# Cross-attention values by seven products of quarters in a Perceiver block on one core

## The reference

```python
q = (query @ Wq + bq).reshape(b, sq, 16, 64)      # query = layernorm(x)
k = (key @ Wk + bk).reshape(b, 512, 16, 64)       # key = value = ctx_1024
v = (value @ Wv + bv).reshape(b, 512, 16, 64)     # Wq, Wk, Wv: 512 x 1024
scores = jnp.einsum('bqhd,bkhd->bhqk', q, k) / 8
attn = jax.nn.softmax(scores, axis=-1)
out = jnp.einsum('bhqk,bkhd->bqhd', attn, v).reshape(b, sq, 1024)
out = out @ Wo + bo + query                       # then a layernorm
```

## Time and profile before

| | |
|---|---|
| median of three runs | 1711.32 us (1709.48 to 1712.38) |
| the profiled execution | 1711.51 us, its span 1709.7 us |
| TensorE busy, of the span | 94% |
| VectorE, ScalarE, GpSimd busy | 68%, 55%, 18% |
| mean granted clock of TensorE | 0.976 |
| first attention's loop | about 75 to 955 us |

### The profile page before, as it was taken

How to read it: one execution, slowest core, us unless ns; L and a number is a source line. 1 busy time by engine, 2 the same in 40 slices (tenths; PEclk the granted TensorE clock), 3 DMA queues, 4 the chain that set the end, 5 groups by cost and what they waited for, 6 DMA issues and landing times. The chain is left out here.

```text
span 1709.7 us, 27478 instructions
## 1 busy us (share of the span) xinstructions
PE 1615.2 (94%) x10730; PEld 1361.0 (80%) x10730; DVE 1163.9 (68%) x1978; ACT 938.0 (55%) x1700; POOL 307.3 (18%) x258
## 2 busy tenths in 40 slices
PE   7999999999999999999999878994899999999987
PEld 6888888888888888888887766773788888888876
DVE  4277777877777777777777666775768448548842
ACT  5466666666666666666666433442656336336631
POOL 4201211011101110111100161565311011101101
PEclk9999999999999999999999999996999999999899
DMA  6601830111101110111002560114757437528711
GB/s 228 212 24 54 131 77 7 54 57 54 37 27 53 57 54 8 54 56 54 7 5 80 173 187 14 55 57 138 249 150 212 141 87 242 155 89 247 221 39 21
DMA packets 54107, 165.21 MB, mean 97 GB/s; under 512 B 10612, under 2 KB 10996, under 8 KB 53408
## 3 DMA queue, kind: packets, MB, share of 16 engines
q1 hardware_dynamic: 38032, 131.88, 22.6%
q0 software_dynamic: 15920, 31.19, 8.7%
HBM read 143.54 MB, written 55.64 MB: 117 GB/s over the span
## 5 line engine op out<-in xcount | busy, mean ns | idle before, releaser
L413 PE MATMUL psum<-ctx,Wk 128*128 128x512 f32 x1536 | 386.2, 400 | 0.0
L413 PE MATMUL psum<-Wv,ctx 128*128 128x512 f32 x1536 | 368.7, 389 | 0.0
L413 PEld LDWEIGHTS psum<-Wv,ctx 128*128 128x128 f32 x1536 | 288.3, 188 | 59.9
L413 PEld LDWEIGHTS psum<-ctx,Wk 128*128 128x128 f32 x1536 | 280.1, 189 | 55.9
L932 DVE SCALAR_TENSOR_TENSOR kT<-psum,bkc,kT 64x512 fp32r<-64x512 f32 x256 | 191.9, 750 | 170.0 <-ACT kT L1322 165.8
L413 PE MATMUL psum<-xgT,Wh 128*128 128x224 f32 (+5 forms) x1536 | 250.0, 316 | 15.1 <-issue 10.2
L413 PEld LDWEIGHTS psum<-xgT,Wh 128*128 128x128 f32 x1536 | 228.4, 196 | 32.7 <-issue 12.6
L766 PE MATMUL psum<-Wh,hs 128*128 128x512 f32 x981 | 245.6, 396 | 0.0
L1332 ACT ACTIVATE Pr<-Pr,smn 128x512 f32<-128x512 f32 x128 | 92.6, 724 | 233.9 <-DVE smn L941 233.9
L1322 ACT ACTIVATE kT<-psum,bkc 64x512 fp32r<-64x512 f32 x256 | 175.1, 684 | 77.7 <-PE psum L413 73.8
L766 PEld LDWEIGHTS psum<-Wh,hs 128*128 128x128 f32 x981 | 181.1, 190 | 33.7 <-DVE hs L1207 0.3
(11 more groups left out here) (154 smaller groups left out, 1911.1 us busy)
## 6 DMA issues: line engine op xcount, KB each, us to landing
raw<-in_W SPq DMA_DIRECT2D x128, 512.0 KB, 4.3
expert_rows<-in_spare_rows SPq DMA_DIRECT2D x16, 1042.0 KB, 7.3
raw<-in_ctxT SPq DMA_DIRECT2D x32, 512.0 KB, 4.4
xg<-expert_rows POOLq DMA_DIRECT2D x32, 256.0 KB, 5.9
low_parts<-Olo POOLq DMA_DIRECT2D x32, 128.0 KB, 2.4
oT<-low_parts SPq DMA_DIRECT2D x8, 512.0 KB, 4.3
out_x<-x SPq DMA_DIRECT2D x12, 256.0 KB, 2.2
xs<-in_x SPq DMA_DIRECT2D x4, 512.0 KB, 6.8
```

The costliest lines, as they stand in the source:

```text
L413: mm = pe.matmul(dst, l, r, start=n == 0, stop=n == len(pairs) - 1)
```

## The change

The values of a batch, 512 keys x 1024 dims, are no longer eight tiles of twelve matmuls. Context and Wv are cut into quarters (256 keys x 256 dims, 256 dims x 512), and each half of the keys' tiles (p = 0, 1; G = 2b + p) gets seven products P1 to P7 of two blocks, six matmuls each, after Strassen and Winograd. Their operands are quarters and sums of quarters: S1 to S4 of the context, made for each batch, and T1 to T4 of Wv, made once, each split in a high and a low part.

- TensorE takes them in the order P1, P6 (in steps with n % 4 = 2), P2, P7 (3), P4, P5 (0), P3 (1), behind `weigh`, alternating between two PSUM banks. No values are projected ahead of the loop.
- ScalarE copies P1 out of PSUM (`move_v`), VectorE adds the others up in the value tiles (`evict_v`): one sum for P6, P2, P7, P4 and P3, two for P5, seven per G. The sums stand ahead of the reciprocal in VectorE's step, as the eviction did.
- VectorE no longer scales the probabilities: ScalarE does, at the end of its step, waiting for the reciprocal (`s_recip`).
- The values have no bias in them. It is added when the weighed output is evicted, in four pieces of 128x64 each on ScalarE (high part, `Ohr`) and VectorE (low part).
- Both parts of the output go to DRAM (`high_parts` beside `low_parts`) and come back by `high_part` and `low_part`, since the keys' weights now lie where `Ohi` is.
- The queries go to DRAM through four staging tiles `qst` (`q_rows`) and come back per batch (`fetch_qb`, `qb`); the score operand is built in halves of a batch, eight copies of 64x256 per batch.
- GpSimd makes S1 to S4 (`ctx_sums`) and their low parts (`sums_low`), eight operations of 128x512 per batch; ScalarE makes their high parts (`sums_high`, in steps with n % 8 = 4, 6 and 7). At the start VectorE and ScalarE do the same for the first batch and for Wv, and VectorE takes over GpSimd's splits there.
- The experts: the first chunk of `weighted` waits for all chunks of its expert but for the last expert's, GpSimd issues a filler copy for each chunk that an expert doesn't have, and the exponential of the router's last tile (`d_gate`) stands ahead of a weight split.

```diff
-        QO = place("QO", c0, [P, NJ, T])
...
+        VW = {name: [place(f"{name}{i}", c0 + kb + 4 * i, [P, 2, 512], F32R) for i in range(2)]
+              for name, kb in (("T1", 32), ("T4", 40), ("B22", 56), ("B11", 64), ("T2", 72), ("B21", 80), ("T3", 88))}
+        qst = [place(f"qst{r}", c0 + 48 + 2 * r, [P, 512]) for r in range(4)]
+        qb = [place(f"qb{r}", c0 + 48 + 2 * r, [P, NJ, TB]) for r in range(2)]
+        Ohr = [place(f"Ohr{r}", c0 + 52 + r, [P, NJ // 2, TB], F32R) for r in range(4)]
...
+        def v_products(n):
+
+            if n < 2:
+                return ((0, "P1"), (0, "P6")) if n == 0 else ((0, "P2"), (0, "P7"), (0, "P4"), (0, "P5"))
+            G, names = {2: ((n + 2) // 4, ("P1", "P6")), 3: ((n + 1) // 4, ("P2", "P7")), 0: (n // 4, ("P4", "P5")), 1: ((n - 1) // 4, ("P3",))}[n % 4]
+            return (((0, "P3"),) if n == 2 else ()) + (tuple((G, name) for name in names) if G < NG else ())
...
+                if t < 2:
+                    sp.wait_ge(v_psum, 7 * NG - 1)
+                    dst = oH[t][:]
+                else:
+                    sp.wait_ge(k_psum, NS)
+                    dst = Ohi[:, :, t * P:(t + 1) * P]
+                sp.dma_start(dst.bitcast(F32), high_parts[t]).then_inc(low_in[t % 4], 16)
...
+                elif name == "P7":
+                    pe.wait_ge(s_lo, 4 * b + 2)
+                    pe.wait_ge(v_done, 7 * G + 1)
+                    left, right = key_tile(CS["S3"], p), "T3"
...
-                products(v_bank(n), split_pairs([pair(ctx[b % 2], slice(None), k, ks) for k in range(KD)],
-                                                      [pair(Wv, slice(None), k, cs) for k in range(KD)])).then_inc(v_psum, 1)
+                    pe.wait_ge(s_lo, 4 * b + 4)
+                    pe.wait_ge(v_done, 7 * G + 4)
+                    left, right = key_tile(CS["S4"], p), "B22"
+                pairs = split_pairs(left, [[VW[right][i][:, kk, :] for i in range(2)] for kk in range(2)])
+                mm = products(v_bank(G, name), pairs)
+                mm.then_inc(v_psum, 1)
...
-            for n in range(HALF):
-                project_v(n)
             for n in range(NS + 3):
                 if n < NS:
                     project_k(n)
                 if 0 <= n - 1 < NS:
                     scores(n - 1)
-                if n + HALF < NS:
-                    project_v(n + HALF)
                 if n >= 6 and n % HALF == 2:
                     weigh(n // HALF - 1)
+                for G, name in v_products(n):
+                    project_v(G, name)
...
+                if name == "P6":
+                    v.wait_ge(v_moved, G + 1)
+                    if v_room(G):
+                        v.wait_ge(o_psum, v_room(G))
+                    v.tensor_tensor(v_tile(G, 0, 1), src, v_tile(G, 1, 0), ALU.add).then_inc(v_done, 1)
...
+                elif name == "P5":
+                    v.wait_ge(v_done, n + 4)
+                    v.tensor_tensor(v_tile(G, 1, 1), src, v_tile(G, 1, 1), ALU.add).then_inc(v_done, 1)
+                    v.tensor_tensor(v_tile(G, 0, 1), src, v_tile(G, 0, 1), ALU.add).then_inc(v_done, 1)
...
-                if n + HALF < NS:
-                    evict_v(n + HALF)
+                for G, name in v_products(n):
+                    evict_v(G, name)
                 if n >= 1:
                     v.wait_ge(s_exp, 3 * m + 3)
                     v.reciprocal(srec[:, r:r + 1], ssum[:, r:r + 1]).then_inc(s_recip, 1)
-                    v.wait_ge(s_recip, m + 1)
-                    v.tensor_scalar(Pr[m % 2][:], Pr[m % 2][:], srec[:, r:r + 1], None, ALU.mult).then_inc(p_done, 1)
-                if j == 2 and b + 1 < B:
-                    build_qbd(b + 1)
+                if n % HALF == 2 and n // HALF + 1 < NS // HALF:
+                    build_qbd(n // HALF + 1)
...
+                    if n >= 4:
+                        s.wait_ge(q_out[n % 4], 16 * (n // 4))
+                    s.activation(qst[n % 4][:], bank[2 + n % 6], ACT.Identity, bias=bqs[:, j:j + 1], scale=SCALE1).then_inc(q_done, 1)
...
+                        s.activation(qs[h][u % 2][dst, :, own], qb[b % 2][own, HALF * half:HALF * (half + 1), :], ACT.Copy).then_inc(qbd_hi, 1)
...
+                for s_ in range(HALF):
+                    high = s.activation(Ohr[u % 4][:, s_, :], bank[7][:, s_ * TB:(s_ + 1) * TB], ACT.Identity,
+                                        bias=bvc[:, HALF * half + s_:HALF * half + s_ + 1])
+                high.then_inc(o_hi, 1)
...
+                    s.activation(v_tile(G, 1, 0), v_bank(G, name), ACT.Copy).then_inc(v_moved, 1)
...
+                for G, name in v_products(n):
+                    move_v(G, name)
+                if n % HALF == 2 and n // HALF + 1 < NS // HALF:
+                    build_qbd(n // HALF + 1)
...
+                if 0 <= n - 1 < NS:
+                    m, r = n - 1, (n - 1) % 3
+                    s.wait_ge(s_recip, m + 1)
+                    s.activation(Pr[m % 2][:], Pr[m % 2][:], ACT.Copy, scale=srec[:, r:r + 1]).then_inc(p_done, 1)
+                if n < NS and b + 1 < B and j in (4, 6, 7):
+                    sums_high(b + 1, {4: ("S2", "S3"), 6: ("S1",), 7: ("S4",)}[j])
...
             x2_turned(NT - 1)
+            d_gate(NT - 1)
             split_first(3)
-            d_gate(NT - 1)
...
+            def ctx_sums(b):
+
+                x0, x1_ = (raw[raw_of[sum_load(b, c)]][:].rearrange("p (a b) -> p a b", a=2) for c in range(2))
+                n = 4 * b
+                g.wait_ge(s_lo, n - 1)
+                g.tensor_tensor(tS[0][:], x0[:, :, 256:512], x1_[:, :, 256:512], ALU.add).then_inc(s_sum, 1)
...
+                    g.wait_ge(s_hi, 4 * b + i + 1)
+                    g.tensor_tensor(CS[name][1][:], src[:], CS[name][0][:], ALU.subtract).then_inc(s_lo, 1)
...
+                g.dma_start(q_rows[n // NJ, n % NJ], qst[n % 4][:]).then_inc(q_out[n % 4], 16)
...
+                for parts, x in ((high_parts, Ohr), (low_parts, Olo)):
+                    g.dma_start(parts[b // 2, :, HALF * half:HALF * (half + 1), b % 2 * TB:(b % 2 + 1) * TB], x[u % 4][:].bitcast(F32)
+                                ).then_inc(low_out[u % 4], 16)
...
-                        v.wait_ge(y_ready, q + c + 1)
+                        v.wait_ge(y_ready, c + 1)
                     elif c == 0:
-                        v.wait_ge(y_ready, q + 1 if q < E else q + CH)
-                    else:
                         v.wait_ge(y_psum, NI * (q + 1))
```

More of the change, by code:

```diff
@@ L62, in perceiver_block @@
         bkc = small("bkc", [P, NJ])
+        bvc = small("bvc", [P, NJ])
         mv = small("mv", [P, NT, 2])
@@ L193, in ctx_load, with sum_load, hi_turn, v_bank @@
             return (L_CTX0 if b == 0 else L_CTX + 2 * (b - 1)) + c
+        def sum_load(b, c):
+            return (L_S0 if b == 0 else L_CTX + 2 * (b - 1)) + c
+        def hi_turn(n):
+            return n + 1 if n < L_WV else n + 1 - (L_CTX - L_WV)
+        VK = (0, 2, 1, 3)
+        NG = 2 * B
+        V_ORDER = ("P1", "P6", "P2", "P7", "P4", "P5", "P3")
+        def v_bank(G, name):
+            return bank[2 + (7 * G + V_ORDER.index(name)) % 2]
+        v_slot = [{}]
+        for b in range(B):
+            first = [v_slot[b][0, kt] for kt in range(NKT)] if b else list(range(4))
+            second = [v_slot[b][1, kt] for kt in range(NKT)] if b else list(range(4, 8))
+            v_slot.append({(g, p + 2 * r): (first, second)[p][2 * r + g] for p in range(2) for r in range(2) for g in range(2)})
+        v_slot = v_slot[1:]
+        def v_tile(G, r, g):
+            b, p = divmod(G, 2)
+            return V[v_slot[b][g, p + 2 * r]][:]
+        def v_room(G):
+            b, p = divmod(G, 2)
+            return (8 * b if p else 8 * b - 4) if b else 0
+        def v_products(n):
[3 more added lines that the diff above has]
+            return (((0, "P3"),) if n == 2 else ()) + (tuple((G, name) for name in names) if G < NG else ())
         def w_load(q, i):
@@ L498, in project_k @@
                     loaded(*range(L_WK, L_WK + 4))
+                    loaded(ctx_load(0, 0), ctx_load(0, 1))
                 if n >= 2:
@@ L553, in c_product @@
                     pe.wait_ge(o_lo, NS // HALF)
-                products(c_bank(t), split_pairs([(Ohi[:, j, rows], oT[t % 4][:, j, :]) for j in range(NJ)],
+                products(c_bank(t), split_pairs([(oH[t][:, j, :] if t < 2 else Ohi[:, j, rows], oT[t % 4][:, j, :]) for j in range(NJ)],
                                                   [pair(Wo, slice(None), j) for j in range(NJ)])).then_inc(c_psum, 1)
-            for n in range(HALF):
-                project_v(n)
             for n in range(NS + 3):
@@ L901, in evict_v @@
[L901 to L909 removed]
+                    q = qs[h][u % 2]
@@ L1582, in gpsimd_program @@
                 if b >= 2:
+                    low_store(2 * b - 4)
+                if b < B:
+                    ctx_sums(b)
+                if b >= 2:
                     low_store(2 * b - 3)
```

(5 more changed lines are left out.)

378 lines of the change are left out of this document (260 added, 118 removed).

## The result

The changed kernel takes 1831.93 us (median of 4 runs, 1829.76 to 1835.28), the kernel before 1711.26 beside it: ratio 1.0708, interval 1.0689 to 1.0727. It is slower by 121 us; the prediction was 1838, 1790 to 1890.

The account below looks back on a forecast made before the run. ScalarE's program-order ring with forced waits was to bound the loop, 63.4 us per eight steps against TensorE's 52.6; 1711.5 plus loop 118, start 2, end 4, loads 4, experts -2 gave 1838 us, range 1790 to 1890.

Parts of the forecast that it names:

- ScalarE's ring: First attention's loop: ScalarE - VectorE - ScalarE in program order, 5.63 us a step, becomes the bound; 1795 to 1885, 76%.
- Eight steps: One batch of the first attention's loop: ScalarE's work and forced waits sum to 63.4 us, against 55.4 before.
- The wait for the reciprocal: ScalarE's scaling waits for VectorE's reciprocal behind the value sums: 0.43 or 1.15, twice each, 3.2 us per batch.
- GpSimd beside the operand's low parts: GpSimd could draw out VectorE's low parts of the score operand: 1.2 us per batch, 18 in all, time 1856.
- The signs: Mid-loop: about 63 us per eight steps, TensorE idle before weighings and turns, ScalarE's key eviction no longer waiting for TensorE.
- Rival (a): Loop: TensorE stays the bound and its 44 us gain arrives, about 1666 us; 4%.
- Rival (b): Loop: ScalarE bounds it but less, reciprocal waits hidden, 59.5 us per batch, about 1775 to 1790; 8%.
- Rival (c): Loop: TensorE's idle gaps cost it its full clock, +80 us, given as about 1900; 10%.
- The start: Before the loop's steady part: early value products leave, sums and zeros replace them; +2 us, ends -5 and +8.
- The loop's sum: Steps 2 to 122: 15 periods at 8.0 us more each, less 2 for the last batch, 118 us.
- The end: End of the loop: value products end two steps later and scalings lie in the last steps; +4 us.
- Loads of high parts: Output projection: 6 x 512 KB more loads, 9 us of DMA, half taken; +4 us, ends 0 and 10.

Follow-up runs that it names:

- e3: The kernel before with only the scaling of the probabilities moved from VectorE to ScalarE; 1714.86 us, ratio 1.0029.
- e6: Changed kernel with scaling and P1's copy on VectorE, P5's second sum later, reciprocal earlier, S1 to S4 high parts on GpSimd; 1749.32 us, ratio 1.0245.
- e2: Changed kernel with VectorE's reciprocal moved ahead, behind the first sum of the values instead of the last; 1800.20 us, ratio 1.0532.
- e4: Changed kernel with 56 instead of 84 value matmuls per eight steps, the left factor's low part left out; 1841.09 us, ratio 1.0764.
- e10: Changed kernel with only the start reordered: first keys evicted right behind the queries, second batch's context split in step 1; 1838.89 us, ratio 1.0747.
- e9: Changed kernel without four loads of high parts; whole time not comparable, first output product to second attention's weights 54.5 us against 59.8.
- e1: Changed kernel with the scaling of the probabilities back on VectorE, right behind the reciprocal; 1760.38 us, ratio 1.0293.

## Why the prediction was right, step by step

The forecast, ScalarE's ring as the bound, is what happened. The 121 us split, by the same event in both traces, into: start +9.1 (third key eviction, 89.00 to 98.11), loop +109.1 (from there to step 122), end +4.2 (to the first output product, 955.78 to 1078.16), output projection and router +4.2 (to the first expert, 1197.12 to 1323.71), experts -5.4 (to the last expert's last down product).

- *Eight steps*: predicted 63.4, measured 62.45. The ring with the scaling is 6.24 in plain steps, so 5.63 and 0.61 were right; e3 shows the same sum in the other kernel. P1's copy 0.48, operand 4 in 1.73 (predicted 8 x 0.43), output 4 in 0.93 (8 x 0.24), high parts 0.52, context 1.89: all within 0.02 a piece. These were read in the rows and not taken out one by one; the scaling, the wait and (in e6) the high parts were.
- *The wait for the reciprocal* was sized too high, 3.2 for 2.45: 1.15 against 1.0 behind three sums, 0.43 against 0.22 behind two. I spaced sums by 0.72; in the step shown above they start 0.80, 0.61 and 0.60 apart, reciprocal included.
- *GpSimd beside the operand's low parts*, the upper end of 1856: it does happen, 1.52 for two instead of 0.85 (at 419.46), but these are not on the ring; with the 2.45 of e2 the sum of the pieces is 62.6 without it. The Trainium skill, "GPSIMD Engine Reference", section 1 (Specifications), from which the prediction took 1856, is borne out for the operation; by the sum, the loop does not pay for it. The same row of that section names VectorE instructions in a 2-port mode beside those with two inputs, which the prediction left out.
- *The signs*: key evictions no longer wait for TensorE, as forecast. TensorE's idle time, 6.6 per eight steps, is only in half where the prediction had it, 2.4 before weighings and 0.9 before turns, put down to ScalarE; 2.4 before scores and 0.9 before value products are put down to VectorE. ScalarE's idle time before the scaling shows behind three sums alone.
- *Rival (a)*, TensorE the bound, falls with e4. *Rival (b)*, 59.5 per eight steps with the waits hidden, is what e2 makes of the kernel: 60.0. *Rival (c)*: the granted clock over the loop is 0.98 against 1.00, and a weighing took 3.01 us at 1004.68 for 2.08 at 1034.96; but e4, at 0.95, has the same loop, so the time is ScalarE's. (This rival's own sum, 1838 + 80, gives 1918, not about 1900.)
- *The start* failed: +2 predicted, ends -5 and +8, measured +9.1. The step that failed is the hand count, by which "the four early value products (11 us) leave the start" and what takes their place costs 2 on balance. In the kernel before, TensorE works through them without a gap (63.87 to 74.75) and has no idle time up to the third keys. In the changed one it does 36 matmuls fewer before the third keys, some 8 us, but now stands idle ahead of them for 5.67 (for the low parts of S1 to S4 on VectorE) and 4.59 us (for the first keys, evicted at 84.88 for 77.67), its query products end 2.9 us later, and part of it runs at half clock (0.50 from 76.6 to 79.4). The hand count, with the second keys at about 82 (measured 86.90) and the third 2.4 later than before, had these waits too short. Of the products that come back, four then stand between the first scores and the third keys' projection. e10 shows that earlier evictions of the first two keys bring the third keys forward by 0.75 only. Rows of the changed kernel:

```profile
76.63 2.93 PE L507 MATMUL psum<-T,S 128*128 128x512 f32 x6 [5.67 <-DVE S L1051]
...
87.40 1.19 PE L637 MATMUL psum<-kT,qs 128*128 128x512 f32 x2 [4.59 <-DVE kT L1111]
88.39 2.64 PE L507 MATMUL psum<-B,ctx 128*128 128x512 f32 x6
90.86 1.55 PE L507 MATMUL psum<-T,S 128*128 128x512 f32 x6
92.34 1.65 PE L507 MATMUL psum<-T,ctx 128*128 128x512 f32 x6
93.83 1.52 PE L507 MATMUL psum<-T,S 128*128 128x512 f32 x6
95.19 2.88 PE L507 MATMUL psum<-ctx,Wk 128*128 128x512 f32 x12
```

- *The loop's sum*: 118 predicted, 109.1 measured. A period grew by 7.09 instead of 8.0, which makes 14 over the 15; the last grew by 2 less than the others, as predicted; but the first, steps 2 to 10, grew by 11.8, 4.7 more than the others, which belongs to the start. So the start was 12 too low and the periods 14 too high: start and loop together 118 against 120, and that the total came so close is in part luck.
- *The end*: +4, measured +4.2. *Loads of high parts*: +4, half of an estimated 9, measured 5.3 (e9). *Gate*: the pause ahead of the first expert shrinks by 2.5 (15.86 to 13.38, start to start), as the -2 had it, and VectorE's wait for the gate's exponential falls from 2.67 to 0.17.
- *The experts' rows themselves* I had at no difference; they take 489.9 us for 495.4. Nearly the same expert code took between 489.9 and 501.1 in the kernels here that send the same rows to the experts. That is not understood: waits for loads differ, and no run tells why. So differences of some 5 us between two of these kernels can't be put down to the loop unless the loop's own rows show them.

## What to carry to other kernels

Ahead of a change that saves work on the busiest engine, follow the next engine's operations in time once round the loop: its reserve is the period less its work and its forced waits, not the idle share of the page, and here it was 5.3 us against 12 us of additions. An operation moved to an engine that stands in such a ring costs its full start-to-start time as soon as the reserve is gone, and a short operation that another engine waits for (the reciprocal) belongs ahead of long ones that nobody waits for (e2), though in e6 its own wait for the exponential then held up VectorE. Where that engine is then relieved, look for the third: with 52.2 us on ScalarE by the sum of its terms and 53.5 of busy time on TensorE the loop still took 56.4, since ScalarE waited for VectorE. Whether the seven products can win on this kernel stays open: no run reached the time before.

## What the runs showed of the hardware

A scaling of 128x512 in fp32 on VectorE, both sides in SBUF, takes 0.49 us alone and up to 1.61 with a GpSimd sum of 1.29 beside it: begun within 0.02 us of that sum, it ends 0.29 us after it (393.67 + 1.60 against 393.69 + 1.29). The same holds for the other long scalings of that kernel (e1): 44 take over 0.65 us, each starts while a GpSimd operation runs or within 0.03 us of its start, and but for one (0.48) each ends 0.28 to 0.29 us behind it. I had expected this of operations with two inputs in SBUF only. The Trainium skill, "SBUF — State Buffer", section "Who interferes with whom", lists such a scaling among the operations that can take both of VectorE's ports and says that against GpSimd the later one blocks until the other is finished. The trace agrees that the scaling waits until GpSimd's operation is finished, and without GpSimd's sums the longest was 0.62; in six of the 44 the scaling's recorded start lies up to 0.03 us ahead of GpSimd's, so which was later is not to be told from the recorded starts there.
